# A graph-attention kernel on one core: scores in two groups of three units, and a new order of the work around them

## The chip, the core and the metric

One NeuronCore of a Trainium2 chip runs the whole kernel. The metric is the device time of one execution in microseconds (us). Five engines are spoken of: PE (TensorE, the matmuls; its weight loads are listed as PEld), DVE (VectorE), ACT (ScalarE), POOL (GpSimd), and SP (SyncE), which here only issues DMAs. Each engine runs its own list of instructions in order, and they meet through semaphores. Matmul results lie in eight PSUM banks of 128 partitions by 512 float32.

## What is computed

32 batches of 256 tokens with 384 features each; six heads of 64 features. The reference, cut to what matters:

```python
q = _heads(seq_inputs @ Wq + bq)
k = _heads(seq_inputs @ Wk + bk)
v = _heads(seq_inputs @ Wv + bv)
scores = jnp.einsum('bhqd,bhkd->bhqk', q, k) / np.sqrt(HEAD_SIZE)
bias = jnp.where(graph_mask, 0.0, NEG)[:, None]
probs = jax.nn.softmax(scores + bias, axis=-1)
ctx = jnp.einsum('bhqk,bhkd->bhqd', probs, v)
...
h = jnp.maximum(_layernorm(x, axis=-1), 0.0)
x = x + _L0_gnn_ref(h, L0_gnn_Wq, L0_gnn_bq, ..., adj)
```

## The kernel before

Every float32 matmul operand is split into an fp16 `hi` and an fp16 `lo` part, and a product is three fp16 matmuls (`three`: hi by hi, hi by lo, lo by hi). The work of a batch `b` is:

- `normalise` (POOL), `h_hi_rows` (ACT), `h_lo_rows` (DVE) and a DMA transpose `transpose_h` (SP) make the normalised input by columns, `h_cols`;
- `project_qk(b, j)`, 18 matmuls of 256 columns, makes q and k of head pair `j` (three pairs). `qk_full` (ACT) copies them out, `qk_hi_part` (DVE, a cast) and `split_lo` (POOL) split them into the tile `split`;
- `project_v(b, t)`, 9 matmuls of 384 columns, makes v of token half `t`; `v_hi_part` (ACT) and `v_lo_part` (DVE) split it;
- a **unit** `u` is one token half `t = u // 3` of one head pair `j = u % 3`, six in a batch. `scores` makes 12 matmuls for two units; each uses 64 of the 128 rows of the array, one for each head of the pair (`a` = 0, 1), and the two run side by side. `mask_and_max` (DVE, two instructions for a unit) masks them, `exps` and `probs_hi` (ACT) and `probs_lo` (POOL) make the probabilities, and `transpose_probs` (SP) turns them by DMA into `p_cols`;
- `apply_probs(b, u)`, 12 matmuls of 64 or 65 columns, sums the context of three units into the single bank `ctx`; `divide(b, t)` (DVE) takes it out, `transpose_context(b, t)` turns it on PE, `context_hi` (ACT) and `context_lo` (DVE) split it, `project_out(b, t)`, again 9 matmuls of 384 columns, multiplies by Wf, and `finish(b, t)` (DVE) adds the residual, which `add_bias` (POOL) has made. `store` (SP) writes it out.

The order on each engine is written out by hand. A start-up is followed by a function `cycle(b)` on each engine for b = 1 to 29, and by a hand-written end for the last two batches, `PREV` (30) and `LAST` (31). On PE a cycle scores batch b in three groups of two units (`scores(b, g)`), applies the last four units of b-1 and the first two of b, and projects b+1. All buffers are shared over batches with two, three or four copies. The score banks are two (`score_bank[a]`), so the next group may be written only when `mask_and_max` has read the one before (`logits_ready`). The first group of a cycle needs the splits of head pairs 0 and 1 (`qk_lo_ready`), the second that of pair 2 as well.

Two waits return below. `apply_probs(b, 0)` and `apply_probs(b, 3)` overwrite the one context bank and so wait for the `divide` before them. And DVE and POOL both read and write SBUF: `qk_hi_part` and `h_lo_rows` last longer beside POOL work.

## Time and profile before

| | us |
|---|---|
| median of 3 runs (589.86 to 590.72) | 590.62 |
| the profiled execution, its own time | 591.8 |
| its span, first to last instruction | 590.0 |
| start-up, until the scores of batch 2 start | 64.0 |
| 28 cycles, batches 2 to 29 | 485.3 |
| the end, from the scores of batch 30 on | 40.8 |
| PE busy share, mean granted clock | 97%, 0.996 |

How to read it: the trace gives each instruction's start and duration. Matmuls overlap, so what one costs is the distance from its start to the next one's start, not its duration. A busy share says little on DVE, ACT and POOL; what matters is whether their chain delivers before PE gets to the instruction that needs it. A cycle here means the time from the first scores matmul of one batch to that of the next.

### The profile page before, as it was taken

How to read it: one execution, taken by the hardware profiler on the slowest of the kernel's cores; microseconds unless marked ns; L12 is line 12 of the kernel's file. 1: busy time of each engine (PE TensorE's matmuls, PEld its weight loads, DVE VectorE, ACT ScalarE, POOL GpSimd, SP SyncE). 2: the span in 40 equal slices, each digit the busy share in tenths (PEclk: the TensorE clock that was granted, in tenths of full speed). 3: DMA queues.
4: the chain of work that ended last, by engine and by line, in shares of the span. 5: the costliest groups of instructions: out<-in, count | busy, mean ns of one | idle time of the engine just before them, and what ended most of it. 6: DMA issues, size and time to landing. Idle time of an engine off the chain costs nothing.

```text
span 590.0 us, 17760 instructions
## 1 busy us (share of the span) xinstructions
PE 573.5 (97%) x6640; PEld 428.9 (73%) x6640; DVE 473.8 (80%) x1484; ACT 516.1 (87%) x1161; POOL 491.3 (83%) x533
## 2 busy tenths in 40 slices
PE   7997999999999999999999999999999999999977
PEld 7676777777777777777777777777777777777755
DVE  4988788888888888878888887887877778787775
ACT  1788999899999999999999999999999999999882
POOL 2779998888998888899888889988888988888960
PEclk9999999999999999999999999999999999999999
DMA  8047889788888978899988877899988788987584
GB/s 273 10 77 140 133 169 184 158 169 167 156 156 165 176 162 168 174 129 174 179 167 170 162 169 150 158 183 156 183 162 159 151 159 181 160 157 143 72 162 117
DMA packets 275641, 92.01 MB, mean 156 GB/s; under 512 B 257634, under 2 KB 275555, under 8 KB 275555
## 3 DMA queue, kind: packets, MB, share of 16 engines
q1 hardware_dynamic: 274352, 90.87, 79.6%
q8 instruction: 53, 0.87, 0.6%
q14 instruction: 34, 0.27, 0.1%
q10 hardware_dynamic: 1202, 0.01, 0.1%
HBM read 17.05 MB, written 12.58 MB: 50 GB/s over the span
## 4 chain that ended last, share of the span: by engine, by line
PE 80%; DVE 6%; ACT 5%; DMA 5%; issue 2%; POOL 2%; ACTq 0%; SPq 0%; DVEq 0%; POOLq 0%
PE ring L1106 18%; PE ring L1108 18%; PE ring L1107 18%; PE scores L1169 11%; PE ctx L1195 5%; PE ring L1207 3%; PE ctx L1197 3%; PE ctx L1196 3%; DMA p_cols<-p_rows 3%; ACT probs L574 2%; DVE logits L796 1%; DVE h_rows L813 1%; DMA bf_row<-in_L_gnn_bf_dram 1%; ACT qk L602 1%; POOL p_rows L440 1%
## 5 line engine op out<-in xcount | busy, mean ns | idle before, releaser
L440 POOL TENSOR_TENSOR p_rows<-probs,p_rows 128x512 f16<-128x512 f32 x190 | 220.6, 1161 | 30.2 <-ACT p_rows L582 29.8
L796 DVE CUSTOM_DVE_ANT_0 logits<-scores,mask,logit_unscale 128x256 f32<-128x256 f32 x384 | 169.1, 478 | 57.5 <-PE scores L1169 57.3
L574 ACT ACTIVATE probs<-logits,raised 128x256 f32<-128x256 f32 x372 | 168.9, 501 | 6.1
L1106 PE MATMUL ring<-h_cols,w_hi 128*128 128x256 f16 x576 | 157.2, 273 | 0.0
L1108 PE MATMUL ring<-h_cols,w_lo 128*128 128x256 f16 x576 | 157.0, 273 | 0.0
L1107 PE MATMUL ring<-h_cols,w_hi 128*128 128x256 f16 x576 | 156.9, 272 | 0.0
L426 POOL TENSOR_TENSOR split<-qk,split 128x512 f16<-128x512 f32 x96 | 111.4, 1160 | 36.4 <-DVE split L820 36.4
L582 ACT ACTIVATE p_rows<-probs 128x512 f16<-128x512 f32 x190 | 119.6, 630 | 5.9
L602 ACT ACTIVATE qk<-ring,qk_bias_s,qkv_ratio 128x256 f32<-128x256 f32 x192 | 96.5, 552 | 3.9 <-PE ring L1108 3.8
L1195 PEld LDWEIGHTS ctx<-v_hi,p_cols 128*128 128x128 f16 x756 | 69.0, 97 | 33.9 <-issue 26.1
L1195 PE MATMUL ctx<-v_hi,p_cols 128*128 128x65 f16 x756 | 88.1, 195 | 5.5 <-DMA p_cols<-p_rows 4.1
L1196 PE MATMUL ctx<-v_lo,p_cols 128*128 128x64 f16 x756 | 87.6, 192 | 0.0
L1197 PE MATMUL ctx<-v_hi,p_cols 128*128 128x65 f16 x756 | 87.6, 193 | 0.0
L820 DVE CAST split<-qk 128x512 f16<-128x512 f32 x96 | 64.8, 675 | 27.4 <-ACT qk L602 27.1
L570 ACT ACTIVATE raised<-least,p_raise 128x2 f32<-128x2 f32 x186 | 54.3, 292 | 32.9 <-DVE least L796 31.8
L1169 PE MATMUL scores<-split 64*128 64x256 f16 x1152 | 79.5, 271 | 3.2 <-DVE least L796 2.5
L1169 PEld LDWEIGHTS scores<-split 64*128 64x128 f16 x1152 | 48.4, 94 | 31.7 <-issue 18.8
L1196 PEld LDWEIGHTS ctx<-v_lo,p_cols 128*128 128x128 f16 x756 | 69.6, 98 | 2.5
L1197 PEld LDWEIGHTS ctx<-v_hi,p_cols 128*128 128x128 f16 x756 | 69.7, 97 | 0.0
L435 POOL TENSOR_TENSOR residual<-x_in,bf_full 128x384 f32<-128x384 f32 x64 | 68.0, 1081 | 0.0
L1106 PE MATMUL ring<-w_hi,h_cols 128*128 128x384 f16 x192 | 62.6, 326 | 0.7 <-DVE w_lo L895 0.7
L1106 PE MATMUL ring<-w_hi,ct_hi 128*128 128x384 f16 x192 | 62.8, 327 | 0.0
(116 smaller groups left out, 1155.7 us busy)
## 6 DMA issues: line engine op xcount, KB each, us to landing
x_in<-in_x_dram SPq DMA_DIRECT2D x32, 384.0 KB, 3.8
out_dram<-result SPq DMA_DIRECT2D x62, 192.0 KB, 2.2
p_cols<-p_rows SPq DMA_TRANSPOSE x190, 3.2
adj_in<-in_adj_dram SPq DMA_DIRECT2D x32, 64.0 KB, 2.6
w_raw<-in_L_gnn_Wq_dram SPq DMA_DIRECT2D x1, 576.0 KB, 6.1
w_raw<-in_L_gnn_Wv_dram SPq DMA_DIRECT2D x1, 576.0 KB, 7.9
w_raw<-in_L_gnn_Wf_dram SPq DMA_DIRECT2D x1, 576.0 KB, 9.0
h_cols<-h_rows SPq DMA_TRANSPOSE x29, 4.8
```

The costliest lines, as they stand in the source:

```text
L426: pool.tensor_tensor(split[b.parity][j][:, 0:4:3, :], qk32[j][:], split[b.parity][j][:, 1:3, :], ALU.subtract).then_inc(qk_lo_ready, 1)
L440: pool.tensor_tensor(p_rows[u][:, 1], probs[u % 3][:], p_rows[u][:, 0], ALU.subtract).then_inc(p_lo_ready, 1)
L574: act.activation(probs[u % 3][:, a], logits[u % 3][:, a], ACT.Exp, bias=raised[u % 3][:, a:a + 1], scale=-1.0).then_inc(probs_ready, 1)
L582: act.activation(p_rows[u][:, 0], probs[u % 3][:], ACT.Copy).then_inc(p_hi_ready, 1)
L796: dve.tensor_tensor_reduce(out=logits[u % 3][:, a], in0=score_bank[a][:, u % 2 * S:(u % 2 + 1) * S], in1=mask[b.parity][:, t], scale=logit ...
L1106: pe.matmul(out_ap, a_hi, m_hi, start=first, stop=False)
L1107: pe.matmul(out_ap, a_hi, m_lo, start=False, stop=False)
L1108: return pe.matmul(out_ap, a_lo, m_hi, start=False, stop=last)
L1169: mm = pe.matmul(score_bank[a][:, u % 2 * S:(u % 2 + 1) * S], tile[own, q, t * P:(t + 1) * P], tile[own, k], start=(n == 0), stop=(n == 2))
L1195: pe.matmul(ctx_ps[:, h], hi, vh, start=(s == 0), stop=False)
L1196: pe.matmul(ctx_ps[:, h, 0:D], hi, vl, start=False, stop=False)
L1197: mm = pe.matmul(ctx_ps[:, h], lo, vh, start=False, stop=(s == QT - 1))
```

## The change

Scores come in two groups of three units. They use three banks, the third being the one that held the peaks of the weights at the start: heads 0 of units 1 and 2 share a bank, heads 1 of units 0 and 1 share another, and the third bank holds head 0 of unit 0 and head 1 of unit 2. These last two lie on different rows of the array, so the first matmul of unit 2's head 1 waits for unit 0's head 0 by a new semaphore, `shared_bank_done`, which PE sets for itself. All three splits of a batch are now needed at the start of its first group. The order in `cycle` is new on every engine: on SP the next input's load is the last of the cycle; on POOL `probs_lo` of unit 0 comes ahead of `root` and `normalise`, and that of unit 2 ahead of `split_lo(b + 1, 0)`, `split_lo(b + 1, 2)` goes ahead of `probs_lo(b, 4)` and `add_bias` last. Batch 1 has a PE order of its own, with a projection between the applied units. Batch 0 is scored in four groups (0 and 1; 2; 3; 4 and 5). The end is in another order too, with other banks for its context and output. In the diff the pieces behind the first `cycles` are, in this order, the cycles of SP, POOL, ACT and DVE, and then PE.

```diff
-    GROUPS = UNITS // 2
+    GROUPS = UNITS // C
...
-        score_bank = [bank("scores0"), bank("scores1")]
-        peak_bank = bank("peaks")
+        score_bank = [bank(f"scores{n}") for n in range(3)]
+        peak_bank = score_bank[2]
...
+        shared_bank_done = sem("shared_bank_done")
...
-        last_pt = {4: ring[2], 5: score_bank[0]}
+        last_pt = {4: ring[2], 5: score_bank[2]}
...
+        def score_of(u, a):
+            n, column = ((1, 0), (2, 0), (0, 0), (2, S), (0, S), (1, S))[u % C * 2 + a]
+            return score_bank[n][:, column:column + S]
...
-            return ring[3] if t == 1 and b.k >= B - 2 else ring[1]
+            return ring[2] if t == 1 and b.k == B - 1 else ring[1]
...
+        def ct_of(b, t):
+            return (score_bank[0] if b.k == B - 1 else ring[1]) if t == 0 else ring[0]
...
-            bank = peak_bank if b.k == B - 1 and t == 0 else ctx_bank
+            bank = ring[3] if b.k == B - 1 and t == 0 else ctx_bank
...
-        def cycles(cycle):
-            for k in range(1, B - 2):
+        def cycles(cycle, first=1):
+            for k in range(first, B - 2):
                 cycle(Batch(k))
...
@@ -325,37 +342,24 @@
...
+                transpose_probs(b + -1, 4)
+                transpose_probs(b + -1, 5)
                 if (b + -2).exists():
                     store(b + -2, 0)
-                if before:
-                    transpose_probs(b + -1, 5)
-                if here:
-                    transpose_probs(b, 0)
+                transpose_probs(b, 0)
                 if (b + -2).exists():
                     store(b + -2, 1)
-                if here and (b + 4).exists():
+                if (b + 3).exists():
+                    wait(sp, mask_ready, (b + 1).count(2, 2))
+                    load_adj(b + 3)
+                transpose_probs(b, 1)
+                transpose_probs(b, 2)
+                transpose_h(b + 2)
+                transpose_probs(b, 3)
+                if (b + 4).exists():
                     wait(sp, residual_ready, b.count(2, 2))
                     load_x(b + 4)
...
@@ -494,40 +498,22 @@
...
+                probs_lo(b, 0)
+                root(b + 2)
+                normalise(b + 2)
+                make_mask(b + 1)
+                probs_lo(b, 1)
+                probs_lo(b, 2)
+                split_lo(b + 1, 0)
+                split_lo(b + 1, 1)
+                probs_lo(b, 3)
+                split_lo(b + 1, 2)
+                probs_lo(b, 4)
+                add_bias(b + 1)
 
...
@@ -671,46 +657,27 @@
...
+                exps(b, 0)
+                probs_hi(b, 0)
+                v_hi_part(b, 1)
+                exps(b, 1)
+                probs_hi(b, 1)
+                qk_full(b + 1, 0)
+                context_hi(b + -1, 0)
+                exps(b, 2)
+                probs_hi(b, 2)
+                h_hi_rows(b + 2)
+                qk_full(b + 1, 1)
+                exps(b, 3)
+                probs_hi(b, 3)
+                qk_full(b + 1, 2)
+                exps(b, 4)
+                context_hi(b + -1, 1)
+                probs_hi(b, 4)
+                exps(b, 5)
+                v_hi_part(b + 1, 0)
+                probs_hi(b, 5)
...
@@ -970,54 +937,34 @@
...
+                context_lo(b + -1, 0)
+                mask_and_max(b, 3)
+                divide(b + -1, 1)
+                h_lo_rows(b + 2)
+                qk_hi_part(b + 1, 1)
                 if (b + 3).exists():
                     layer_stats(b + 3, (1,))
+                mask_and_max(b, 4)
+                if (b + 3).exists():
                     layer_moments(b + 3)
-                if here:
-                    mask_and_max(b, 5)
-                if before:
-                    finish(b + -1, 0)
-                    context_lo(b + -1, 1)
+                qk_hi_part(b + 1, 2)
+                mask_and_max(b, 5)
+                context_lo(b + -1, 1)
+                finish(b + -1, 0)
 
...
-            def scores(b, g):
-                for u in (2 * g, 2 * g + 1):
+            def scores(b, units):
+                for u in units:
                     if u < C:
                         wait(pe, qk_hi_ready, b.count(C, u + 1))
                         wait(pe, qk_lo_ready, b.count(C, u + 1))
-                wait(pe, logits_ready, b.count(2 * UNITS, 4 * g))
-                for u in (2 * g, 2 * g + 1):
+                wait(pe, logits_ready, b.count(2 * UNITS, 2 * units[0]))
+                for u in units:
                     t, tile = u // C, split[b.parity][u % C]
                     for n, (q, k) in enumerate(((1, 2), (1, 3), (0, 2))):
                         for a in range(2):
+                            if u % C == 2 and n == 0 and a == 1:
+                                wait(pe, shared_bank_done, b.count(GROUPS, u // C + 1))
                             own = slice(D * a, D * a + D)
-                            mm = pe.matmul(score_bank[a][:, u % 2 * S:(u % 2 + 1) * S],
-                                           tile[own, q, t * P:(t + 1) * P], tile[own, k],
+                            mm = pe.matmul(score_of(u, a), tile[own, q, t * P:(t + 1) * P], tile[own, k],
                                            start=(n == 0), stop=(n == 2))
+                            if u % C == 0 and n == 2 and a == 0:
+                                mm.then_inc(shared_bank_done, 1)
                 mm.then_inc(scores_ready, 1)
...
-                if t == 0 and (b + -1).exists():
-                    wait(pe, result_ready, (b + -1).count(2, 2 if b.k < B - 1 else 1))
+                if t == 0 and b.k == B - 1:
+                    pe.wait_ge(logits_ready, b.count(2 * UNITS, 2 * UNITS))
+                elif t == 0 and (b + -1).exists():
+                    wait(pe, result_ready, (b + -1).count(2, 2))
...
-            scores(Batch(0), 1)
+            scores(Batch(0), (2,))
             project_v(Batch(0), 1)
             bias_product(range(1, C))
             project_qk(Batch(1), 0)
             pe.wait_ge(peak_ready, 6)
             pe.wait_ge(peaks_joined, 2)
-            spread_peaks(peak_bank, slice(5, 6))
+            spread_peaks(ring[1], slice(5, 6))
+            scores(Batch(0), (3,))
             project_qk(Batch(1), 1)
-            scores(Batch(0), 2)
+            scores(Batch(0), (4, 5))
             project_qk(Batch(1), 2)
...
+            scores(Batch(1), (0, 1, 2))
+            apply_probs(Batch(0), 2)
+            project_qk(Batch(2), 0)
+            apply_probs(Batch(0), 3)
+            project_qk(Batch(2), 1)
+            apply_probs(Batch(0), 4)
+            transpose_context(Batch(0), 0)
+            scores(Batch(1), (3, 4, 5))
+            apply_probs(Batch(0), 5)
+            project_qk(Batch(2), 2)
+            apply_probs(Batch(1), 0)
+            pe.wait_ge(w_lo_ready, 8)
+            project_out(Batch(0), 0)
+            project_v(Batch(2), 0, (0,))
+            apply_probs(Batch(1), 1)
+            transpose_context(Batch(0), 1)
+            project_v(Batch(2), 0, (1, 2))
+            project_v(Batch(2), 1)
...
+                scores(b, (0, 1, 2))
+                apply_probs(b + -1, 2)
                 if (b + -2).exists():
                     project_out(b + -2, 1)
...
+                apply_probs(b + -1, 3)
+                project_qk(b + 1, 0)
+                apply_probs(b + -1, 4)
+                transpose_context(b + -1, 0)
+                project_qk(b + 1, 1)
+                scores(b, (3, 4, 5))
+                apply_probs(b + -1, 5)
+                project_qk(b + 1, 2)
+                apply_probs(b, 0)
+                project_out(b + -1, 0)
+                project_v(b + 1, 0, (0,))
+                apply_probs(b, 1)
+                transpose_context(b + -1, 1)
+                project_v(b + 1, 0, (1, 2))
+                project_v(b + 1, 1)
+            cycles(cycle, 2)
...
 
-            scores(PREV, 0)
+            scores(PREV, (0, 1, 2))
             apply_probs(PREV + -1, 2)
             project_qk(LAST, 0)
             project_out(PREV + -2, 1)
-            scores(PREV, 1)
+            scores(PREV, (3, 4, 5))
             apply_probs(PREV + -1, 3)
+            apply_probs(PREV + -1, 4)
             transpose_context(PREV + -1, 0)
-            apply_probs(PREV + -1, 4)
             project_qk(LAST, 1)
             apply_probs(PREV + -1, 5)
-            scores(PREV, 2)
             project_qk(LAST, 2)
             transpose_context(PREV + -1, 1)
+            project_v(LAST, 0, (0,))
             project_out(PREV + -1, 0)
-            project_v(LAST, 0, (0,))
+            project_v(LAST, 0, (1, 2))
+            scores(LAST, (0, 1, 2))
+            project_v(LAST, 1)
             apply_probs(PREV, 0)
-            scores(LAST, 0)
-            project_v(LAST, 0, (1, 2))
             apply_probs(PREV, 1)
-            project_v(LAST, 1)
             apply_probs(PREV, 2)
             project_out(PREV + -1, 1)
-            scores(LAST, 1)
+            scores(LAST, (3, 4, 5))
+            apply_probs(PREV, 3)
             transpose_context(PREV, 0)
-            scores(LAST, 2)
-            apply_probs(PREV, 3)
             apply_probs(PREV, 4)
+            project_out(PREV, 0)
             apply_probs(PREV, 5)
-            project_out(PREV, 0)
-            transpose_context(PREV, 1)
             apply_probs(LAST, 0)
             turn_probs(4)
+            transpose_context(PREV, 1)
+            apply_probs(LAST, 1)
             turn_probs(5)
-            apply_probs(LAST, 1)
             apply_probs(LAST, 2)
             project_out(PREV, 1)
```

Where the order moved, first **PE at the start of a cycle**: the end of `project_v`, the scores, and the first matmul of `apply_probs`. Before:

```order
L1108 MATMUL ring<-w_hi,h_cols 128x384
L1169 MATMUL scores<-split_0 128x256 [waits qk_lo_ready,qk_hi_ready,logits_ready]
L1169 MATMUL scores<-split_0 128x256 x5
L1169 MATMUL scores<-split_1 128x256 x6
L1195 MATMUL ctx<-v_hi,p_cols 128x65 [waits p_placed2]
```

And after:

```order
L1055 MATMUL ring<-w_hi,h_cols 128x384
L1120 MATMUL scores<-split_0 128x256 [waits qk_hi_ready,qk_lo_ready,logits_ready]
L1120 MATMUL scores<-split_0 128x256 x5
L1120 MATMUL scores<-split_1 128x256 x6
L1120 MATMUL scores<-split_2 128x256
L1120 MATMUL scores<-split_2 128x256 [waits shared_bank_done]
L1120 MATMUL scores<-split_2 128x256 x4
L1147 MATMUL ctx<-v_hi,p_cols 128x65 [waits p_placed2]
```

The third unit has joined the group, with a wait on PE's own semaphore between its first two matmuls.

Second, **DVE after the second group of the new cycle** (L763 is `mask_and_max`, L780 `h_lo_rows`, L787 `qk_hi_part`, L800 and L802 `divide`), from unit 3 to the cast of pair 2:

```order
L763 ISA logits0,least0<-scores1,mask1,logit_unscale 128x256
L763 ISA least0 128x1
L763 ISA logits0,least0<-scores2,mask1,logit_unscale 128x256
L763 ISA least0 128x1
L800 RECIPROCAL inv_sum1<-ctx 128x6
L802 TENSOR_TENSOR context1<-ctx,inv_sum1 128x384
L780 SCALAR_TENSOR_TENSOR h_rows<-normed,h_rows 128x3x128 x2
L787 CAST split0_1<-qk32_1 128x512
L826 BN_STATS stats<-x_in2 128x6
```

Before, the two `h_rows` instructions stood ahead of unit 3:

```order
L820 CAST split0_0<-qk32_0 128x512
L841 TENSOR_TENSOR ct_lo0<-ring1,ct_hi0 128x384
L813 SCALAR_TENSOR_TENSOR h_rows<-normed,h_rows 128x3x128 x2
L796 ISA logits0,least0<-scores0,mask1,logit_unscale 128x256
```

They now stand behind unit 3 and its `divide`, and ahead of the casts of pairs 1 and 2.

Third, **POOL in the second half of a cycle** (the lines with `p_rows` are `probs_lo`, those with `split1` are `split_lo`). Before:

```order
L440 TENSOR_TENSOR p_rows1<-probs1,p_rows1 128x512
L426 TENSOR_TENSOR split1_0<-qk32_0,split1_0 128x2x256
L440 TENSOR_TENSOR p_rows2<-probs2,p_rows2 128x512
L426 TENSOR_TENSOR split1_1<-qk32_1,split1_1 128x2x256
L440 TENSOR_TENSOR p_rows3<-probs0,p_rows3 128x512
L435 TENSOR_TENSOR residual3<-x_in3,bf_full 128x384 x2
L440 TENSOR_TENSOR p_rows4<-probs1,p_rows4 128x512
```

After:

```order
L444 TENSOR_TENSOR p_rows1<-probs1,p_rows1 128x512
L444 TENSOR_TENSOR p_rows2<-probs2,p_rows2 128x512
L430 TENSOR_TENSOR split1_0<-qk32_0,split1_0 128x2x256
L430 TENSOR_TENSOR split1_1<-qk32_1,split1_1 128x2x256
L444 TENSOR_TENSOR p_rows3<-probs0,p_rows3 128x512
L430 TENSOR_TENSOR split1_2<-qk32_2,split1_2 128x2x256
```

The split of pair 2 has moved up behind unit 3, and the residual has left the place between units 3 and 4 for the end of the cycle.

## Rows read from the trace of the kernel before

**Rows 1.** The page: busy us, share of the span and instructions of each engine

```profile
PE 573.5 (97%) x6640; PEld 428.9 (73%) x6640; DVE 473.8 (80%) x1484; ACT 516.1 (87%) x1161; POOL 491.3 (83%) x533
```

**Rows 2.** Windows: length; busy of PE, PEld, DVE, ACT, POOL; clock, DMA, GB/s

```profile
0.00:64.00 64.00, 55.17 (x505) 43.72 (x507) 50.58 (x145) 43.61 (x93) 44.39 (x60) 0.97 0.57 127
64.00:549.20 485.20, 484.22 (x5713) 360.38 (x5712) 396.12 (x1254) 445.55 (x1010) 425.38 (x449) 1.00 0.85 163
549.20:590.00 40.80, 34.06 (x426) 24.76 (x425) 27.09 (x85) 26.99 (x60) 21.53 (x26) 0.99 0.61 118
```

**Rows 3.** PE timeline (start, duration, what): first scores of batches 1, 2, 30

```profile
44.16 0.83 PE L1169 MATMUL scores<-split 64*128 64x256 f16 x12
...
63.96 0.83 PE L1169 MATMUL scores<-split 64*128 64x256 f16 x12
...
549.22 0.83 PE L1169 MATMUL scores<-split 64*128 64x256 f16 x12
```

**Rows 4.** PE timeline around the second scores group of batch 15

```profile
294.33 0.27 PE L1107 MATMUL ring<-h_cols,w_hi 128*128 128x256 f16 x1
294.44 0.27 PE L1108 MATMUL ring<-h_cols,w_lo 128*128 128x256 f16 x1
294.65 0.83 PE L1169 MATMUL scores<-split 64*128 64x256 f16 x12
295.41 0.20 PE L1195 MATMUL ctx<-v_hi,p_cols 128*128 128x65 f16 x1
```

**Rows 5.** DVE timeline in batch 15's cycle, in brackets the idle time before

```profile
295.52 0.48 DVE L796 CUSTOM_DVE_ANT_0 logits<-scores,mask,logit_unscale 128x256 f32<-128x256 f32 x1 [1.02 <-PE scores L1169]
...
298.25 1.43 DVE L813 SCALAR_TENSOR_TENSOR h_rows<-normed,h_rows 128x384 f16<-128x384 f32 x2
299.60 0.47 DVE L796 CUSTOM_DVE_ANT_0 logits<-scores,mask,logit_unscale 128x256 f32<-128x256 f32 x1
...
300.41 0.18 DVE L833 RECIPROCAL inv_sum<-ctx 128x6 f32<-128x6 f32 x1
...
301.10 0.42 DVE L820 CAST split<-qk 128x512 f16<-128x512 f32 x1
...
303.42 0.73 DVE L820 CAST split<-qk 128x512 f16<-128x512 f32 x1 [0.64 <-ACT qk L602]
304.07 0.55 DVE L859 BATCH_NORM_STATS2 stats<-x_in 128x6 f32<-128x384 f32 x1
304.54 0.29 DVE L865 BATCH_NORM_AGGREGATE mean_var<-stats 128x2 f32<-128x6 f32 x2
...
305.02 0.48 DVE L796 CUSTOM_DVE_ANT_0 logits<-scores,mask,logit_unscale 128x256 f32<-128x256 f32 x1
```

**Rows 6.** Operations of one tile: least, median and greatest duration in ns

```profile
L813 DVE SCALAR_TENSOR_TENSOR h_rows<-normed,h_rows x58: 543/580/1555, 53.8 to 541.3; 128x384 f16<-128x384 f32 x58
...
L820 DVE CAST split<-qk x96: 416/729/1311, 20.2 to 567.0; 128x512 f16<-128x512 f32 x96
L426 POOL TENSOR_TENSOR split<-qk,split x96: 1142/1158/1472, 20.7 to 567.9; 128x512 f16<-128x512 f32 x96
```

**Rows 7.** Landing time of `p_cols` over the run; PE timeline in batch 1's cycle

```profile
DMA to landing us min/median/max: 3.0/3.2/5.7
...
51.82 0.20 PE L1195 MATMUL ctx<-v_hi,p_cols 128*128 128x65 f16 x1 [1.79 <-DMA p_cols<-p_rows]
```

**Rows 8.** SP timeline at 46 us: the load of batch 4, then two transposes

```profile
45.71 0.37 SPq L283 DMA_DIRECT2D x_in<-in_x_dram  x1
46.13 2.90 SPq L297 DMA_TRANSPOSE p_cols<-p_rows  x2
```

**Rows 9.** Chain that ended last, from 549 us: the transpose of batch 30's unit 5

```profile
570.86 4.75 DMA p_cols<-p_rows
```

**Rows 10.** ACT and PE timelines: last exponentials; `apply_probs` of batch 31's unit 3

```profile
575.16 1.71 ACT L722 ACTIVATE probs<-logits,raised 128x256 f32<-128x256 f32 x4
...
581.28 0.19 PE L1195 MATMUL ctx<-v_hi,p_cols 128*128 128x65 f16 x1
```

249 lines of the change are left out of this document (63 added, 186 removed).

## The prediction, made before the changed kernel was run

> **What bounds the kernel now.** First the shares of busy time: PE 97%, ACT 87%, POOL 83%, DVE 80% [rows 1]. Such a share says little alone, so the windows by stage come next [rows 2]: over the 28 cycles of batches 2 to 29, PE is busy 484.2 of 485.2 us, at full clock. In the start-up it is busy 55.2 of 64.0, in the end 34.1 of 40.8. So 28 cycles are bound by what PE has to stream, and start-up and end hold some 16 us in which PE waits. Third, the starts of the first scores group of a batch [rows 3]: 63.96 for batch 2, 549.22 for batch 30, which is 485.26 / 28 = 17.33 us a cycle; batch 1 starts at 44.16, so its cycle takes 19.80. Last, PE's timeline around a scores group [rows 4]. The projection's matmuls start 0.11 us apart, but the scores start 0.21 after the last of them: 0.10 is lost on the way in. The group runs from 294.65 to the next start at 295.41, 0.76 us, while its six pairs at 0.11 are 0.66: 0.10 is lost on the way out. A group costs 0.20 us beside its work, and nothing hides that on the engine that bounds.
>
> **The cycle: one group fewer.** The same 36 score matmuls come in two groups. That takes away 0.20 us in each of 28 cycles, 5.6 us. The new cycle is 17.13 by the mean (17.33 less 0.20), if everything PE needs is in time. PE's order with starts from the first scores, made of the spacings (scores of three units 1.08, a head pair's projection 1.97, a value or output projection 1.47, `apply_probs` 0.36): `apply_probs(b-1, 2)` at 1.1, `project_out(b-2, 1)` 1.4, `apply_probs(b-1, 3)` 2.9, `project_qk(b+1, 0)` 3.3, `apply_probs(b-1, 4)` 5.2, `project_qk(b+1, 1)` 6.0, the second scores 8.05, `apply_probs(b-1, 5)` 9.1, `project_qk(b+1, 2)` 9.5, `apply_probs(b, 0)` 11.5, `project_out(b-1, 0)` 11.8, `apply_probs(b, 1)` 13.8, and the next batch's scores at 17.1.
>
> **The wait that moves up.** The first group now needs the split of head pair 2, which before was wanted only 5 us later. It hangs on DVE's new order behind the second scores. DVE sees a two-unit group 0.87 after its start (294.65 to 295.52 [rows 4, 5]), so a three-unit one after 0.87 + 3 x 0.11 = 1.20: 8.05 + 1.20 = 9.25. Then by starts [rows 5]: unit 3 0.81 (299.60 to 300.41), `divide` 0.69 (300.41 to 301.10), `h_lo_rows` 1.35 (298.25 to 299.60), cast of pair 1 0.34 (0.42 less the 0.08 by which neighbours overlap), one batch norm 0.47, unit 4 0.81, moments 0.48, together 4.95: 14.20. The cast of pair 2 takes 0.73 beside POOL, and 0.07 to POOL's start: 15.00. The split takes 1.16 [rows 6], 0.06 to PE: 16.2. PE wants it at 17.1: 0.9 us to spare. On the same engine unit 5, which frees the banks, is read by 14.20 + 0.65 + 0.81 + 0.15 = 15.8: 1.3 to spare. ACT is busy 445.55 / 28 = 15.9 of the 17.1 [rows 2] and stays below; POOL 425.38 / 28 = 15.2. `v_lo_part(b, 0)`, which frees the bank of `project_qk(b+1, 1)`, now stands behind unit 2: 1.20 + 3 x 0.81 + `divide` 0.69 + `finish` about 0.53 + its own 0.61 = 5.5 against 6.0. Nothing in the cycle is late by this, and what is queued behind the new wait on PE (all of the cycle) loses nothing.
>
> **The wait inside a group.** PE now waits for its own matmul: unit 0's last product for head 0 is the third pair, at 0.22, and its end is seen some 0.31 after its start (0.87 less the 0.55 at which the last pair of a two-unit group starts): 0.53. The waiting matmul is the seventh pair, at 0.66, and its weights load 0.11 ahead, at 0.55. No row shows such a wait, so bounds: 0 if the 0.02 holds; 0.10 if the array has to run empty once more, the price of leaving a group. The least is 0, since no work goes. I take 0, as the sum of the rows comes out just in time; 0.10 would be 2 x 28 x 0.10 = 5.6 us. The added increment costs no more: the last projection of a head pair carries one too, and its successor is not held. The Trainium skill (TensorE: Matmul & The Clock Gate, The cost: per-tile semaphore tail) says that increments of tiles serialise, about 26 ns each; by that, an estimate, 56 more of them would cost 1.5 us and the sum end at 582.5.
>
> **The SP queue.** The load of x moves from ahead of `transpose_probs(b, 1)` to behind `transpose_probs(b, 3)`, and so ahead of `transpose_probs(b, 4)`. That one is issued about 0.7 into the next cycle and wanted at 5.2, 4.5 later. Transposes land after 3.0 to 5.7, median 3.2 [rows 7]; the 5.7 is just of this kind, issued 0.42 behind a load of x [rows 8] and landing as 51.82 shows [rows 7]. Now the load is 1.3 ahead of it, so I take 4.0 and a late one here and there, 0.2 us in all; the ends are 0 and, if every one took 5.7, 1.2 x 28 = 34 us.
>
> **Start-up.** In batch 1's cycle PE now has two projections between units 2 and 4 of batch 0, where it stood for `divide` and for the late transpose of unit 4. The work of that cycle is 17.1 less the missing `project_out` of 1.5, 15.6. What stays: the transpose of unit 4, whose place on SP does not change, lands at 51.8, 7.7 after the cycle's start, while PE would be there at 5.7 without waits; of these 2.0 us, 1.2 go to `v_lo_part(1, 0)`, now behind unit 2, ahead of it. 15.6 + 2.0 = 17.6, and 0.2 for batch 0's extra group: 17.8 against 19.80, **2.0 us less**. It could be 1.0 (if the slowest `h_rows`, 1.555 us each [rows 6], comes again) or 3.5 (if the transpose landed in 3.2).
>
> **The end.** Before, the chain stands on the transpose of batch 30's unit 5, issued at 570.86 and landing 4.75 later [rows 9]. It is 21.6 us after batch 30's first scores. Now `probs_hi(PREV, 5)` comes ahead of the exponentials of batch 31, and the chain runs through ACT: from 2.2 us (1.20 for the scores, 1.0 for the first unit) six units of exponentials (1.27) with `probs_hi` (0.54), three `qk_full` (0.90), five copies (0.41), six exponentials of batch 31 (0.93; the last two in 1.71 [rows 10]) and four `probs_hi`, about 10.9 + 2.7 + 2.0 + 5.4 + 2.2 = 23.2: done at 25.4 if ACT never waits, against 575.16 + 1.71 - 549.22 = 27.65 now. Behind it stand PE's transpose, two applied units and a `project_out`, as now, until unit 3 of batch 31 at 581.28 - 549.22 = 32.1; what follows that is unchanged. So at most 2.3 us from this chain, and as the row of `p_cols` shows that landings go over 4, I take **2.0 us**; ends 0 and 4.
>
> **Sum.** 5.6 + 2.0 + 2.0 - 0.2 = 9.4 us. The profiled execution took 591.8 (span 590.0), so 582.4 for such a one; it lies 1.2 above the median of 590.62. Against the median: 581.2.
>
> **Rivals.** (A) *POOL beside DVE makes the split late.* `h_rows` takes 0.58 in the median and 1.555 at most, the cast 0.42 to 1.31 [rows 6]. In the rows of DVE the first of two `h_rows` took 0.97 (1.43 and the overlap of 0.08, less the free 0.54). If the second does too, +0.43, and the casts take 1.00 each (between the median of 0.73 and the most), +0.58 and +0.27, the split is there at 17.5, 0.4 late: 28 x 0.4 = 11.2 us, 592.4 and slower. It decides from 0.3 of lateness in each cycle, which eats the whole gain; against it speaks the 0.9 to spare, and that POOL itself waits for the cast of pair 1 and so leaves it alone. 8%. (A2) *Each cast is held for a whole POOL operation*: 1.16 ahead of the free 0.42 for both, 1.16 + 0.85 more than in the walk, 18.2, 1.1 late, 28 x 1.1 = 31 us and 612. Against it: the median of the casts is 0.73, so most are held for 0.3. 2%. The Trainium skill (SBUF — State Buffer, SBUF: two separate sides) gives the rule for this: the port that DVE shares with POOL is locked for a whole instruction and the other engine blocks. (B) *Transposes behind the load of x are late*, by 0.3 a cycle: 8.4 more, 589.6. For it the 5.7 [rows 7]; against it the wider distance. 8%. (C) *The wait inside a group costs* 0.1 each: 5.6 more, 586.8. 10%. (D) *Only the cycle gains*: in start-up and end other waits take the place of those removed, 4.0 more, 585.2. 12%. That the change doesn't do what it says is excluded by PE's order, which shows the groups.
>
> **How the numbers follow.** The forecast has 60%, with 577.0 to 585.0 for its own ends (2 us either way in start-up and end each never fall together, plus the odd landing). 577 to 588 holds nearly all of it with (C) and (D), 8 in 10. A measurement of this kernel can tell about 0.2%, 1.2 us, from no change. Faster by that, under 589.4: the forecast, (C), (D) and half of (B), 86%; within it, the other half of (B) and a little of (A), 5%; slower, the rest of (A) and (A2), 9%.
>
> **What would show it.** A cycle of 17.1 us between first scores, two groups with 0.1 lost on each side, PE's waits for `split` absent. Wrong if PE's list of waits names `split`, `least` or `p_cols` in the middle window for more than 3 us; if pairs six and seven of a group stand over 0.12 apart; if batch 1's cycle is over 18.5, or the end over 39.5.

## The result, and the profile of the changed kernel

The changed kernel takes 592.40 us (median of 6 runs, 592.12 to 593.62), the kernel before, run beside it, 590.65. The ratio is 1.0031, with a 95% interval of 1.0017 to 1.0046. So it is slower by 0.3%, where 581.2 was forecast, and outside the range of 577 to 588. The profiled execution has a span of 590.5 us against 590.0 before.

First the page's shares, to be held against [rows 1]:

```profile
PE 569.0 (96%) x6640; PEld 434.4 (74%) x6640; DVE 479.8 (81%) x1484; ACT 509.8 (86%) x1161; POOL 491.1 (83%) x533
```

TensorE is busy 4.5 us less (573.5 before), as part of the time lost around a group counts as busy and there are fewer groups, but the span has not shrunk with it. Where it went is in the windows by stage (length; then busy time of PE, PEld, DVE, ACT, POOL; clock, DMA share, GB/s), to be held against [rows 2]:

```profile
0.00:62.73 62.73, 54.97 (x503) 43.28 (x503) 49.78 (x145) 43.57 (x93) 43.18 (x59) 0.97 0.53 123
62.73:550.79 488.06, 480.13 (x5713) 366.27 (x5713) 402.79 (x1254) 439.14 (x1009) 424.92 (x449) 1.00 0.88 162
550.79:590.50 39.71, 33.87 (x426) 24.89 (x425) 27.23 (x85) 27.14 (x61) 23.05 (x27) 1.00 0.72 127
```

In the middle window PE is busy 480.13 of 488.06 us, so it now stands still for 7.9 us, against 1.0 before. The stage's borders are the first scores of batches 1, 2 and 30 on PE's timeline, as in [rows 3] (the last projection ahead of batch 2's is shown too):

```profile
43.80 0.39 PE L1120 MATMUL scores<-split 64*128 64x256 f16 x4
...
62.48 0.33 PE L1055 MATMUL ring<-w_hi,h_cols 128*128 128x384 f16 x1
62.73 0.39 PE L1120 MATMUL scores<-split 64*128 64x256 f16 x4
...
550.79 0.39 PE L1120 MATMUL scores<-split 64*128 64x256 f16 x4
```

| stretch | before | forecast | after |
|---|---|---|---|
| to batch 1's first scores | 44.16 | 44.16 | 43.80 |
| batch 1's cycle | 19.80 | 17.8 | 18.94 |
| cycles 2 to 29, mean | 17.33 | 17.13 | 17.43 |
| from batch 30's first scores to the end | 40.8 | 38.8 | 39.7 |

(The 17.8 holds 0.2 for batch 0's extra group.) The span that was forecast is 590.0 less 9.4, and the measured one, 590.5, is 9.9 us longer. Of these, 28 x 0.30 = 8.4, less the 0.2 that the forecast gave to the SP queue, lie in the cycles: 8.2. PE's list of waits in that window (who waited for whom: us in total, times, longest) names two causes:

```profile
PE scores L1120 <- POOL split L430: 5.0, 20, 0.3
PE ctx L1147 <- DMA p_cols<-p_rows: 2.9, 6, 0.6
```

Twenty of 28 times a batch's first scores wait for POOL's low part of the split, and six times the value products wait for a transpose. The prediction named both kinds of wait as its refutation ("for more than 3 us"); the first is over that alone. Two more of its signs came as well: batch 1's cycle is over 18.5 and the end over 39.5. PE's timeline at the second scores of batch 14 and at the first ones of batch 15:

```profile
279.91 1.16 PE L1120 MATMUL scores<-split 64*128 64x256 f16 x18
281.00 0.20 PE L1147 MATMUL ctx<-v_hi,p_cols 128*128 128x65 f16 x1
...
288.65 0.33 PE L1055 MATMUL ring<-w_hi,h_cols 128*128 128x384 f16 x1
289.23 0.39 PE L1120 MATMUL scores<-split 64*128 64x256 f16 x4 [0.26 <-POOL split L430]
```

The three-unit group runs from 279.91 to 281.00, 1.09 us: nine pairs at 0.11 are 0.99, and 0.10 is lost on the way out. That is what the forecast had (1.08). The wait inside the group stands ahead of the seventh pair, and in all 56 groups of the 28 cycles the trace has that pair 0.109 to 0.110 us behind the sixth, no farther than the other pairs are apart: it costs nothing. But the first scores of batch 15 start 0.58 us after the last projection, where those of batch 2 start 0.25 after it (62.48 to 62.73). Batch 14's first scores were at 289.23 - 17.37 = 271.86. Twenty of the 28 cycles take 17.36 or 17.37; one in which nothing is late takes 17.05. So the scores are 0.32 us late.

DVE's and POOL's timelines between the two groups tell why (rows of DVE, then of POOL; the rows x2 are two instructions in one):

```profile
281.11 0.48 DVE L763 CUSTOM_DVE_ANT_0 logits<-scores,mask,logit_unscale 128x256 f32<-128x256 f32 x1 [0.54 <-PE scores L1120]
...
282.63 2.00 DVE L780 SCALAR_TENSOR_TENSOR h_rows<-normed,h_rows 128x384 f16<-128x384 f32 x2
284.55 0.42 DVE L787 CAST split<-qk 128x512 f16<-128x512 f32 x1
284.88 0.55 DVE L826 BATCH_NORM_STATS2 stats<-x_in 128x6 f32<-128x384 f32 x1
285.35 0.47 DVE L763 CUSTOM_DVE_ANT_0 logits<-scores,mask,logit_unscale 128x256 f32<-128x256 f32 x1
...
286.15 0.24 DVE L832 BATCH_NORM_AGGREGATE mean_var<-stats 128x2 f32<-128x6 f32 x2
286.43 0.92 DVE L835 TENSOR_SCALAR var_s<-mean_var 128x2 f32<-128x2 f32 x1
287.26 0.15 DVE L837 TENSOR_SCALAR neg_mean<-mean_var 128x2 f32<-128x2 f32 x1
287.33 0.41 DVE L787 CAST split<-qk 128x512 f16<-128x512 f32 x1
```

```profile
282.59 1.15 POOL L430 TENSOR_TENSOR split<-qk,split 128x512 f16<-128x512 f32 x1
285.04 1.16 POOL L430 TENSOR_TENSOR split<-qk,split 128x512 f16<-128x512 f32 x1 [1.30 <-DVE split L787]
286.16 1.16 POOL L444 TENSOR_TENSOR p_rows<-probs,p_rows 128x512 f16<-128x512 f32 x1
287.82 1.16 POOL L430 TENSOR_TENSOR split<-qk,split 128x512 f16<-128x512 f32 x1 [0.50 <-DVE split L787]
```

POOL's split of pair 0 starts 0.04 us ahead of DVE's first `h_rows`, and the two `h_rows` take 1.92 us to the next start instead of about 1.0. It is the first one alone that is held: over the cycles the first takes 1.53 us in the median and the second 0.55. POOL's `p_rows` of unit 3 starts at 286.16, and `var_s`, a `tensor_scalar` of two numbers in each partition, starts at 286.43 and ends at 287.35, with POOL's operation (287.32). The batch norm beside POOL's split (284.88) and the unit's logits, which read PSUM, take no longer than elsewhere. Both delays lie ahead of the cast of pair 2, and POOL's split of pair 2 waits for that cast: POOL stands idle 0.50 us just ahead of it, so POOL's own work is not what makes it late. This is not an accident of one cycle, as the operations' durations over the middle of the run show (least/median/greatest in ns; the kernel before first, then the changed one):

```profile
L868 DVE TENSOR_SCALAR var_s<-mean_var x27: 168/170/903, 79.2 to 529.8; 128x2 f32<-128x2 f32 x27
```

```profile
L780 DVE SCALAR_TENSOR_TENSOR h_rows<-normed,h_rows x55: 544/707/1536, 73.5 to 544.5; 128x384 f16<-128x384 f32 x55
L835 DVE TENSOR_SCALAR var_s<-mean_var x27: 912/919/925, 77.3 to 530.7; 128x2 f32<-128x2 f32 x27
L787 DVE CAST split<-qk x82: 411/415/429, 70.0 to 541.0; 128x512 f16<-128x512 f32 x82
```

`var_s` went from 170 ns to 919, in every batch. The casts, for which the prediction feared POOL, went the other way, from 729 [rows 6] to 415. The Trainium skill (SBUF — State Buffer, Who interferes with whom) says which DVE operations want the ports that POOL uses: those with two inputs in SBUF against a POOL operation that reads it, and copies, casts and `tensor_scalar` where they enter a two-port mode; whoever starts first has them for the whole instruction. The rows agree: `h_rows` and `var_s` are held until POOL's operation ends, the logits and the statistics are not. `var_s` is over 0.03 us behind that end; `h_rows`, which takes 0.55 by itself, 0.4 us behind it.

### The profile page after: what moved, and what is told of

It reads as the page before. It is cut to its first block, busy times and chain, and to the rows that moved or that the text cites. A ratio compares the mean times of both kernels' runs of the same rounds, so it can differ in the third digit from the quotient of the medians.

```text
span 590.5 us, 17761 instructions
## 1 busy us (share of the span) xinstructions
PE 569.0 (96%) x6640; PEld 434.4 (74%) x6640; DVE 479.8 (81%) x1484; ACT 509.8 (86%) x1161; POOL 491.1 (83%) x533
## 3 DMA queue, kind: packets, MB, share of 16 engines
HBM read 17.05 MB, written 12.58 MB: 50 GB/s over the span
## 4 chain that ended last, share of the span: by engine, by line
PE 50%; DVE 17%; POOL 14%; issue 9%; DMA 7%; ACT 1%; ACTq 0%; POOLq 0%; DVEq 0%
PE ring L1053 10%; PE ring L1055 10%; PE ring L1054 10%; PE scores L1120 9%; DMA p_cols<-p_rows 6%; DVE logits L763 5%; POOL p_rows L444 5%; POOL split L430 4%; DVE h_rows L780 3%; PE ctx L1147 3%; DVE split L787 2%; POOL residual L439 2%; PE ring L1161 2%; DVE context L802 2%; PE ctx L1149 2%
## 5 line engine op out<-in xcount | busy, mean ns | idle before, releaser
L763 DVE CUSTOM_DVE_ANT_0 logits<-scores,mask,logit_unscale 128x256 f32<-128x256 f32 x384 | 168.6, 477 | 48.7 <-PE scores L1120 48.6
L1120 PE MATMUL scores<-split 64*128 64x256 f16 x1152 | 74.4, 270 | 5.8 <-POOL split L430 5.6
L787 DVE CAST split<-qk 128x512 f16<-128x512 f32 x96 | 41.9, 436 | 41.5 <-ACT qk L588 41.4
L1120 PEld LDWEIGHTS scores<-split 64*128 64x128 f16 x1152 | 53.3, 94 | 27.5 <-issue 24.2
L439 POOL TENSOR_TENSOR residual<-x_in,bf_full 128x384 f32<-128x384 f32 x64 | 62.8, 1003 | 0.0
```

Source lines behind the costliest of these rows:

```text
L763: dve.tensor_tensor_reduce(out=logits[u % 3][:, a], in0=score_of(u, a), in1=mask[b.parity][:, t], scale=logit_unscale[:, 0:1], scalar=FAR, ...
L1120: mm = pe.matmul(score_of(u, a), tile[own, q, t * P:(t + 1) * P], tile[own, k], start=(n == 0), stop=(n == 2))
```

## Experiments

The theory (T): POOL's operations hold `h_lo_rows` and `var_s`, so that the split of pair 2 comes 0.32 us after TensorE wants it. Rivals: (R1) the wait inside a three-unit group, or the group itself, eats the gain; (R2) late transposes on the reordered SP queue. Each edit is against the changed kernel, if nothing else is said. Ratios are to the kernel before, run on the same chip beside them (its medians there were 590.65 beside after, 591.15 beside e1 to e4, 592.57 beside e5, e6, f1 and f2, 591.52 beside the others), with the 95% interval; compare rows by their ratios. The usual cycle is the commonest distance between the first scores of two batches in the profiled execution.

| kernel | median us | ratio | usual cycle | waits for the split of pair 2 |
|---|---|---|---|---|
| after | 592.40 | 1.0031 [1.0017, 1.0046] | 17.36 | 20 |
| e1, wait for pair 2 two units later | 588.31 | 0.9949 [0.9930, 0.9969] | 17.05 | none |
| e2, moments behind unit 5 | 589.17 | 0.9971 [0.9953, 0.9988] | 17.09 | none listed |
| e3, SP's order as before | 593.78 | 1.0042 [1.0028, 1.0055] | 17.36 | 19 |
| e4, POOL's split of pair 0 short | 585.99 | 0.9905 [0.9878, 0.9931] | 17.05 | none |
| e5, only `var_s`, `neg_mean` later | 591.74 | 0.9991 [0.9972, 1.0010] | 17.23 | 0.19 each |
| e7, POOL's `p_rows` of unit 3 short | 585.32 | 0.9891 [0.9859, 0.9923] | 17.05 | none |
| e6, e1 and unit 1's transpose first | 583.69 | 0.9853 [0.9824, 0.9883] | 17.05 | none |
| e8, e6 with one more group | 595.99 | 1.0071 [1.0047, 1.0094] | 17.62 | none |
| f1, e6 with DVE and ACT reordered | 601.95 | 1.0156 [1.0132, 1.0181] | 17.83 | none |
| f2, f1 with the load of x later | 601.93 | 1.0156 [1.0131, 1.0180] | 17.83 | none |
| g1, e6 with the load of x later | 580.45 | 0.9814 [0.9789, 0.9840] | 17.05 | none |
| g2, g1 with start-up and end changed | 581.62 | 0.9827 [0.9802, 0.9852] | 17.05 | none |

**e1: the wait for pair 2 stands before unit 2.**

```diff
-                for u in units:
-                    if u < C:
-                        wait(pe, qk_hi_ready, b.count(C, u + 1))
-                        wait(pe, qk_lo_ready, b.count(C, u + 1))
                 wait(pe, logits_ready, b.count(2 * UNITS, 2 * units[0]))
                 for u in units:
+                    if u < C:
+                        wait(pe, qk_hi_ready, b.count(C, u + 1))
+                        wait(pe, qk_lo_ready, b.count(C, u + 1))
```

> The changed kernel, with TensorE's waits for the split of head pair j moved from the head of the scores group to just before unit j's own matmuls, so the wait for pair 2 stands two units, 2 x 0.33 = 0.66 us, later. Theory T (the split of pair 2 is 0.32 us late, since DVE's chain behind the second scores is held by POOL): the stall at the start of a batch's first scores is covered, so the usual cycle falls from 17.36 to 17.04 us, and 28 cycles with the odd late transpose take 21 to 28 times 0.32 = 7 to 9 us less: 583.5 to 586 us. Rival R1 (the wait of a matmul inside the group for its own group's matmul is what costs, or the three-unit group itself): nothing changes, 592. Rival R2 (late transposes): the usual cycle stays 17.36, 592.

Measured: 588.31 us, and the usual cycle is 17.05. PE's list of waits in the 28 cycles has one line left:

```profile
PE ctx L1146 <- DMA p_cols<-p_rows: 5.1, 9, 0.8
```

The stall at the scores is gone, by 0.32 a cycle as expected, so R1 falls: the same groups with the same own-semaphore wait run in 17.05. The total gained 4.1 us by the medians (4.8 by the ratios) and not 7 to 9, as the late transposes went from 2.9 us in six waits to 5.1 in nine. From start to start, the value products of unit 1 lose 3.1 us, about as in the changed kernel (3.3), and those of unit 4 lose 3.8, where they lost 0.9. Unit 4's products stand behind the scores that were late, so that lateness had given its transpose 0.32 us more.

**e2: the moments leave the chain.**

```diff
                 mask_and_max(b, 4)
-                if (b + 3).exists():
-                    layer_moments(b + 3)
                 qk_hi_part(b + 1, 2)
                 mask_and_max(b, 5)
+                if (b + 3).exists():
+                    layer_moments(b + 3)
```

> The changed kernel, with layer_moments(b+3) moved on DVE from behind unit 4's mask_and_max to behind unit 5's, so that the two aggregations and the two tensor_scalars, one of which lasts 0.92 us beside a POOL operation, no longer stand ahead of the cast of pair 2. Theory T: the cast then starts when ACT's qk of pair 2 is there, up to 1.2 us earlier, so the first scores are in time: cycle 17.05, 583.5 to 586 us; unit 5 comes no later. Within T, if the held h_lo_rows alone is the cause and ACT's qk is the later one, it gains nothing. Rivals R1 and R2: no change, 592.

Measured: 589.17 us, usual cycle 17.09; the mean cycle is 17.34, with nine odd ones up to 18.46 from transposes (5.9 us). That is the theory's cycle within 0.04; the total again falls short of it by the transposes. The place shows the contention from its other side, on POOL's and then DVE's timeline:

```profile
303.25 1.43 POOL L444 TENSOR_TENSOR p_rows<-probs,p_rows 128x512 f16<-128x512 f32 x1
304.64 1.15 POOL L430 TENSOR_TENSOR split<-qk,split 128x512 f16<-128x512 f32 x1
```

```profile
303.25 0.41 DVE L787 CAST split<-qk 128x512 f16<-128x512 f32 x1
304.39 0.23 DVE L832 BATCH_NORM_AGGREGATE mean_var<-stats 128x2 f32<-128x6 f32 x2
304.66 1.16 DVE L835 TENSOR_SCALAR var_s<-mean_var 128x2 f32<-128x2 f32 x1
```

Here the cast and POOL's `p_rows` start together, and it is POOL that takes 0.27 us more while the cast has its free 0.41. `var_s` then starts just behind POOL's split and lasts 1.16, the whole of it.

**e3: SP's cycle in the order of before.**

```diff
+                if (b + 4).exists():
+                    wait(sp, residual_ready, b.count(2, 2))
+                    load_x(b + 4)
+                transpose_probs(b, 1)
+                transpose_probs(b, 2)
+                transpose_h(b + 2)
                 if (b + 3).exists():
                     wait(sp, mask_ready, (b + 1).count(2, 2))
                     load_adj(b + 3)
-                transpose_probs(b, 1)
-                transpose_probs(b, 2)
-                transpose_h(b + 2)
                 transpose_probs(b, 3)
-                if (b + 4).exists():
-                    wait(sp, residual_ready, b.count(2, 2))
-                    load_x(b + 4)
```

> The changed kernel, with the order of the SP queue's cycle as in the kernel before: the load of x ahead of the transpose of unit 1, the load of adj ahead of that of unit 3. Theory T: the usual cycle stays at 17.36; of the 0.07 us a cycle that lies above it (the odd wait for p_cols, 2 us in all) some may go or come; 590 to 594 us. Rival R2 (what the reordered queue costs is what eats the gain): the cycle falls to 17.1, 585 us.

Measured: 593.78 us, usual cycle 17.36, 19 waits for the split and 5.1 us of waits for transposes. The old order of the queue is no faster here, so R2 falls as the main cause. The trace also has each transpose's time from issue to landing. With the load of x back ahead of unit 1's transpose, that one takes 3.7 us in the median (3.3 in the changed kernel), and unit 4's, which the load has left, 3.05 (3.8 in the changed kernel).

**e4: POOL's split of pair 0 made short** (most of the low parts of pair 0 are left out).

```diff
+                n = 32 if j == 0 and 1 < b.k < B - 2 else S
-                pool.tensor_tensor(split[b.parity][j][:, 0:4:3, :], qk32[j][:], split[b.parity][j][:, 1:3, :],
-                                   ALU.subtract).then_inc(qk_lo_ready, 1)
+                pool.tensor_tensor(split[b.parity][j][:, 0:4:3, 0:n], qk32[j][:, :, 0:n],
+                                   split[b.parity][j][:, 1:3, 0:n], ALU.subtract).then_inc(qk_lo_ready, 1)
```

> The changed kernel, with POOL's low part of the split of pair 0 cut in the cycles from 256 to 32 columns of each half, so that the low parts of most keys and queries of pair 0 are left out: POOL's operation falls from 1.16 to about 0.2 us. Theory T: the first h_lo_rows, which starts beside it, falls from 1.5 to about 0.6 us, the split of pair 2 comes up to 0.9 us earlier, and the first scores are in time: cycle 17.05 us, 583.5 to 586 us; if the 0.92 of the tensor_scalar stays and takes the saving, the cycle stays at 17.36. Rivals R1 and R2: no change, 592.

**e7: POOL's `p_rows` of unit 3 made short** (most of its low parts are left out), the same for the other collision.

```diff
+                n = 32 if u == 3 and 1 < b.k < B - 2 else S
-                pool.tensor_tensor(p_rows[u][:, 1], probs[u % 3][:], p_rows[u][:, 0],
-                                   ALU.subtract).then_inc(p_lo_ready, 1)
+                pool.tensor_tensor(p_rows[u][:, 1, :, 0:n], probs[u % 3][:, :, 0:n], p_rows[u][:, 0, :, 0:n],
+                                   ALU.subtract).then_inc(p_lo_ready, 1)
```

> The changed kernel (without the late wait), with POOL's low part of unit 3's probabilities cut in the cycles from 256 to 32 columns of each half, so that most of those low parts are left out: the POOL operation beside which DVE's var_s lasts 0.92 us falls from 1.16 to about 0.3. Theory T (whatever DVE issues while that POOL operation runs is held to its end): var_s takes 0.2 to 0.4, the cast behind it stays at 0.42, the split of pair 2 comes 0.5 to 0.7 earlier and the cycle of 17.36 becomes 17.05: 586 to 588 us with the odd late transposes. Rival (the two small operations are slow by themselves in this place, for instance as they wait for the aggregation's result): var_s stays at 0.92 and the cycle at 17.36, 592 us.

Measured: 585.99 and 585.32 us, both with a usual cycle of 17.05 and no wait for the split. In e4 the first `h_rows` of a cycle falls from 1.53 to 0.68 us, while `var_s` stays at 0.92; in e7 it is `h_rows` that stays, at 1.53. The row of `h_rows` in e4 (both of a cycle together), and that of `var_s` in e7:

```profile
L781 DVE SCALAR_TENSOR_TENSOR h_rows<-normed,h_rows x56: 543/549/1524, 73.4 to 540.5; 128x384 f16<-128x384 f32 x56
```

```profile
L836 DVE TENSOR_SCALAR var_s<-mean_var x27: 168/170/171, 77.2 to 523.6; 128x2 f32<-128x2 f32 x27
```

DVE's own instructions, their order and their shapes are those of the changed kernel; only a POOL operation got shorter, and `var_s` is back at 170 ns (below the 0.2 to 0.4 expected). So it is not slow by its place or its inputs. Each collision costs more than the 0.32 us by which the split is late, so it takes both to make it late, and taking either away suffices. As part of POOL's work is left out, the totals are no version to use.

**e5: only the two small operations move behind the cast.**

```diff
-                dve.wait_ge(moments, b.count(4, 4))
-                wait(dve, norm_ready, b.count(2, 0))
+                if b.k < 4:
+                    layer_scalars(b)
+
+            def layer_scalars(b):
+
+                dve.wait_ge(moments, b.count(4, 4))
+                wait(dve, norm_ready, b.count(2, 0))
...
                 qk_hi_part(b + 1, 2)
+                if (b + 3).exists():
+                    layer_scalars(b + 3)
                 mask_and_max(b, 5)
```

> The changed kernel, with only the two small tensor_scalars of layer_moments(b+3) (var_s and neg_mean; one lasts 0.92 us where 0.17 is its free time) moved behind the cast of pair 2 on DVE; the aggregations stay, and so does the h_rows of 1.5 us beside POOL's split of pair 0. Theory T: the chain gets 0.9 to 1.0 us shorter, so the split of pair 2 is in time in every cycle: the cycle of 17.36 becomes 17.05, and with the odd late transposes as in the two kernels before the total is 586 to 589 us. Rival: the small operation takes the delay only in place of the cast behind it (POOL's p_rows operation has to end anyway before DVE goes on), so the cast of pair 2 lasts 0.75 longer instead: the cycle stays at 17.36 and the total at 592.

Measured: 591.74 us, usual cycle 17.23. The rival had the mechanism and came within 0.3 us of the total; the 586 to 589 of the theory was wrong. DVE's timeline in one cycle:

```profile
304.64 0.24 DVE L832 BATCH_NORM_AGGREGATE mean_var<-stats 128x2 f32<-128x6 f32 x2
304.80 1.29 DVE L787 CAST split<-qk 128x512 f16<-128x512 f32 x1
```

The cast takes 1.29 us instead of 0.41: it has stepped into the place of `var_s` beside POOL's `p_rows`, which runs from 304.66 to 305.82, and is done 0.27 us behind its end. Only `var_s`'s and `neg_mean`'s own time, some 0.13 of the cycle, is saved, and the waits for transposes ate it (5.0 us in nine, against 2.9 in six). So the delay belongs to the moment, not to the instruction; `var_s` was merely the first that wanted the ports. What helped was a cast that starts no later than POOL's operation (e2), or a shorter POOL operation (e4, e7).

**e6: e1, with unit 1's probabilities and their transpose first.**

```diff
-                make_mask(b + 1)
                 probs_lo(b, 1)
+                make_mask(b + 1)
...
+                transpose_probs(b, 1)
                 if (b + 3).exists():
                     wait(sp, mask_ready, (b + 1).count(2, 2))
                     load_adj(b + 3)
-                transpose_probs(b, 1)
```

> The late wait of e1, and on POOL the low part of unit 1's probabilities ahead of the mask, on SP its transpose ahead of the load of adj, so that this transpose is issued some 1.1 us earlier in each cycle. Theory U (the late wait gave back less than 9 us because transposes that land after 4.4 to 5 instead of 3.2 us are late for the value products of unit 1 by 0.65 to 0.96, five times, and for unit 4 by 0.3 to 0.9, six times): the five of unit 1 go, 4 us, and the 1.36 us for which TensorE waits for the same unit in batch 1's cycle: 588.3 - 5 = 583 us. Rival: the slow landings follow what else the queues carry and fall on the next transpose instead (units 2, 4): 586 to 588 us.

Measured: 583.69 us. The waits for transposes in the 28 cycles are 2.5 us in four, three of them for unit 4, one for unit 2 and none for unit 1, and the cycle of batch 1 takes 18.02 instead of 19.14 in e1. The rival, that a slow landing would fall on the next transpose instead, holds for one of 0.6 us.

**g1: e6, with the load of x behind unit 4's transpose**, and the statistics that need it later on DVE.

```diff
                 transpose_probs(b + -1, 4)
+                if (b + 3).exists() and b.k > 1:
+                    load_x(b + 3)
                 transpose_probs(b + -1, 5)
...
                 transpose_probs(b, 3)
                 if (b + 4).exists():
                     wait(sp, residual_ready, b.count(2, 2))
-                    load_x(b + 4)
...
-                if (b + 3).exists():
-                    layer_stats(b + 3, (0,))
                 qk_hi_part(b + 1, 0)
                 v_lo_part(b, 1)
                 if b.k == 1:
                     weights_lo(3, 8)
                 context_lo(b + -1, 0)
+                if (b + 3).exists():
+                    layer_stats(b + 3, (0,))
```

> The kernel with the late wait and unit 1 first (583.7 us), with the load of x issued behind unit 4's transpose instead of ahead of it, and the statistics that need it behind context_lo(b-1, 0) on DVE. Theory U (unit 4's transpose is slow since it runs beside the 384 KB of x): its landing falls from 3.7 to 3.1-3.3 us, the waits for it (0.94, 0.42 and 1.10 and some small ones in the cycles) go, and the total is 580.5 to 581.5 us. Rival: they are slow by what else the queues carry, and the waits stay or move to units 0 and 5: 583.5 us.

Measured: 580.45 us, 0.9814 of the kernel before and just where it was expected. Its middle window, and all that PE waited for in it:

```profile
62.89:540.90 478.01, 477.65 (x5714) 364.67 (x5714) 405.89 (x1256) 439.91 (x1011) 426.06 (x450) 1.00 0.92 166
```

```profile
PE ctx L1147 <- DMA p_cols<-p_rows: 0.2, 1, 0.2
```

PE is busy 477.65 of 478.01 us, and 478.01 / 28 = 17.07 is the cycle: the one fewer group is now worth its full 28 x 0.20 and somewhat more (17.33 - 17.07 = 0.26, since the odd late cycles of before went too). This is the fastest version of all that were run.

It also shows one cause of slow transposes. In e6 unit 4's takes 3.7 us in the median from issue to landing and 5.1 at most; here, with the load of x behind it, 3.06 and 3.6. Units 5 and 0, which now come next behind the load, go from 3.05 and 3.1 to 3.95 and 4.1, and PE hardly waits for them. Before the change it was unit 1's, just behind the load, that took 4.2.

**g2: g1, with two more edits.**

```diff
                 divide(b + -1, 0)
+                if b.k == 1:
+                    v_lo_part(b, 0)
                 mask_and_max(b, 1)
...
                 mask_and_max(b, 2)
-                v_lo_part(b, 0)
+                if b.k > 1:
+                    v_lo_part(b, 0)
...
+            apply_probs(PREV, 5)
             project_out(PREV, 0)
-            apply_probs(PREV, 5)
```

> g1 with two more edits: in batch 1's cycle v_lo_part(1, 0) ahead of unit 1 on DVE, so that TensorE's wait of 1.21 us for it at 47.5 goes; at the end apply_probs(30, 5) ahead of project_out(30, 0), where TensorE waited 0.97 us. Expected: the first gives 0.5 to 1.2 us unless the late unit 4 of batch 0 takes it back (TensorE waits for its transpose right behind, 1.0 us; then 0); the second 0 to 0.8: together 0.5 to 1.5 us below g1, 580 us. Rival: both waits only move behind, no gain over g1.

Measured: 581.62 us, an interval that overlaps that of g1, and the cycle of batch 1 takes 18.26 against 18.25. The rival holds: PE no longer waits for `v_lo_part(1, 0)`, and waits that much more for the transposes of batch 0. The end takes 39.35 against 39.25: the wait ahead of `project_out(30, 0)` shrinks by 0.6 us, and the next one for a transpose grows by 0.5.

**e8: one more group per cycle**, on e6.

```diff
-                wait(pe, logits_ready, b.count(2 * UNITS, 2 * units[0]))
+                wait(pe, logits_ready, b.count(2 * UNITS, 2 * (units[0] if b.k < 2 else units[0] // C * C)))
...
-                mm.then_inc(scores_ready, 1)
+                if b.k < 2 or units[-1] % C == C - 1:
+                    mm.then_inc(scores_ready, 1)
...
-                scores(b, (0, 1, 2))
+                scores(b, (0, 1))
                 apply_probs(b + -1, 2)
+                scores(b, (2,))
```

> The kernel with the late wait and unit 1 first (583.7 us), with its first scores group cut in two by apply_probs(b-1, 2) between units 1 and 2, both parts released together at the end, so that only one more change between scores and other matmuls is made per cycle. Theory (a group costs 0.20 us beside its work): the cycle goes from 17.05 to 17.25, 28 x 0.20 = 5.6 us more, 589.3 us. Rival (part of what a group costs is taken by its releases and not by the change of shape): less than 0.10 a cycle, 583.7 to 586.5 us. DVE sees the group 0.56 later, which may add late cycles: above 591 would show that.

Measured: 595.99 us, cycle 17.62, 0.57 more than e6. The late cycles that the expectation allowed for came in every one. PE's waits in the 28 cycles:

```profile
PE ctx L1147 <- DVE context L802: 6.1, 28, 0.2
```

DVE sees the group 0.56 us later and its `divide` is late for `apply_probs(b-1, 3)`. From start to start PE loses 0.38 there in each cycle (the list counts 0.22 of it as idle, since the last matmul's tail counts as busy). 0.57 - 0.38 = 0.19 is left for the group itself: the 0.20 of the forecast, shown now by adding one.

**f1 and f2: DVE's cycle reordered**, on e6; f2 has g1's edit besides.

```diff
-                h_lo_rows(b + 2)
                 qk_hi_part(b + 1, 1)
-                if (b + 3).exists():
-                    layer_stats(b + 3, (1,))
+                h_lo_rows(b + 2)
                 mask_and_max(b, 4)
-                if (b + 3).exists():
-                    layer_moments(b + 3)
                 qk_hi_part(b + 1, 2)
                 mask_and_max(b, 5)
+                if (b + 3).exists():
+                    layer_stats(b + 3, (1,))
+                    layer_moments(b + 3)
                 context_lo(b + -1, 1)
...
                 exps(b, 4)
-                context_hi(b + -1, 1)
                 probs_hi(b, 4)
+                context_hi(b + -1, 1)
```

> e6 with DVE's and ACT's order changed as well: the cast of pair 1 ahead of h_lo_rows (it then stands at 12 us of the cycle, beside no POOL operation of its own making), statistics and moments behind unit 5, ACT's context_hi(b-1, 1) behind unit 4's probs_hi. Theory T and U: no chain behind the second scores is late any more, and unit 4's transpose is issued 0.4 to 0.5 us earlier, which takes most of its six late ones (3.5 us) away: 580 to 583 us. Rival: h_rows, later by 0.4, make the transpose of h late, or the moments behind unit 5 push context_lo(b-1, 1) past TensorE's project_out(b-1, 1) at 1.4 of the next cycle: 585 to 590 us.

> f1 with the load of x issued behind unit 4's transpose instead of ahead of it, and the first statistics of x, which need it, behind context_lo(b-1, 0). Theory U: unit 4's transpose, which lands after 3.7 us with the load ahead of it, lands after 3.1 to 3.3, so that its late ones go wholly: 580 to 581 us; unit 5's, behind the load now, has 5 us to spare. Rival: the load then slows unit 0's and unit 5's transposes, with no gain over f1, or statistics wait for x: 583 us.

Measured: 601.95 and 601.93 us. PE's waits in f1 name the reason:

```profile
PE ring L1052 <- DVE result L817: 15.8, 26, 1.1
PE ctx L1145 <- DMA p_cols<-p_rows: 0.6, 1, 0.6
```

`project_out(b-1, 1)`, 1.4 us into the next cycle, waits for `finish(b-1, 0)`, the last in DVE's cycle, which the statistics and moments now push back. I had named the neighbour, `context_lo`, as the rival's cause, and taken 585 to 590 for its price; it was 18 us. The totals tell nothing of f2's load, as both hang on this one wait. The landings do, and as in g1: unit 4's transpose takes 4.0 us in the median in f1 and 3.07 in f2, unit 5's 3.1 and 3.8.

## Why the prediction was wrong, point by point

**One group fewer, 5.6 us: right.** The three-unit group takes 1.09 us, and a cycle in which nothing is late takes 17.05 against 17.26 to 17.30 in most cycles of before. e8 prices a group at 0.19 by adding one.

**The wait inside a group, 0: right.** e1 keeps it and loses nothing. The 17.05 is 17.26 less 0.21. The prediction counted 56 increments more; each cycle has two of `shared_bank_done` more but one of `scores_ready` less, so 28 more. By the Trainium skill (TensorE: Matmul & The Clock Gate, The cost: per-tile semaphore tail), at about 26 ns each, 56 would have cost an estimated 1.5 us (and the sum would have been 582.7, not 582.5), and 28 an estimated 0.7. No run here shows such a cost, and 0.03 us a cycle is too little for these rows to exclude it.

**The split of pair 2 at 16.2 of 17.1: this step failed.** It came at 17.37, and PE wanted it at 17.05. The walk had the right order and the right start: second scores at 8.05 (279.91 - 271.86), DVE's start at 9.25 (281.11). By its terms, read from the timelines above:

| term | forecast | measured |
|---|---|---|
| `h_lo_rows`, two | 1.35 | 1.92 (282.63 to 284.55) |
| moments | 0.48 | 1.18 (286.15 to 287.33) |
| cast of pair 2, to POOL's start | 0.80 | 0.49 (287.33 to 287.82) |
| POOL's split, to PE's start | 1.22 | 1.41 (287.82 to 289.23) |

+0.57, +0.70, -0.31 and +0.19 are +1.15, and with rounding that is 17.37. The two large ones are POOL's work beside DVE; e4 takes away the first of them and e7 the second, and either alone brings back the cycle of 17.05. The mistake was to read a duration off an operation in the old order and to carry it into the new one. `var_s` was taken at its usual 0.17, without asking what POOL does at that time in the new order, and `h_rows` and the casts at what POOL had made of them before. The rival (A) had the mechanism, the place and by luck the very total, 592.4, with 8%. Its sum put the delay on the casts, which came out free, and on the second `h_rows`, where the first alone is held, longer. Against itself it said that POOL leaves the chain alone as it waits for pair 1's cast; POOL does wait for it, and then runs two operations in a row, the second beside `var_s`. The 0.06 us from POOL's end to PE's start had no row behind it and is 0.25. 20 x 0.32 = 6.4 us is the price, more than the 5.6 us that one group fewer gives.

**The SP queue, 0.2: this step failed too.** The sum of cycles 2 to 29 holds 488.06 - 28 x 17.05 = 10.7 us above the undisturbed ones, of which 6.4 are the split and 4.3 odd late transposes, where before had 485.26 - 28 x 17.26 = 2.0 us above its undisturbed cycles. 3.3 of the 4.3 are unit 1's transpose, whose neighbour on SP is now the load of adj. That transpose was not costed: issued 9.67 into the cycle it lands in the usual 3.3 at 13.0, and PE wants it at 13.8, so one that takes 4.7 is late; the longest took 4.8. The other 0.9 are unit 4's, behind the load of x, for which the 0.2 stood. The landing that the prediction took, 4.0, was near (3.8 in the median, 5.1 at most). But in e1, with no stall at the scores, it is issued 1.2 into the next cycle and not 0.7, so it has 4.05 us and not 4.5; there unit 4 costs 3.8 us and unit 1 3.1. So the late split hid part of this error: with the split in time and nothing else changed, e1 takes 588.31, which is also outside the range. Rival (B), transposes behind the load of x, was right in kind and at 0.9 us here and 3.8 in e1 too dear at 8.4. e6 issues unit 1's earlier, g1 besides takes the load from ahead of unit 4's, and the listed waits come to 0.2 us.

**Start-up, -2.0: got -0.9 in batch 1's cycle.** Another 0.4 lies ahead of it (44.16 to 43.80), but kernels with the same start-up code have 43.5 to 44.2 there, so that is not shown to be a gain. The list of PE's idle times in batch 1's cycle, on its timeline:

```profile
48.80 0.28 PE L1053 MATMUL ring<-h_cols,w_hi 128*128 128x256 f16 x1 [1.05 <-DVE v_lo L791]
...
55.80 0.19 PE L1147 MATMUL ctx<-v_hi,p_cols 128*128 128x65 f16 x1 [0.61 <-DVE context L802]
...
59.47 0.20 PE L1147 MATMUL ctx<-v_hi,p_cols 128*128 128x65 f16 x1 [1.20 <-DMA p_cols<-p_rows]
```

From start to start PE loses 1.2 us for `v_lo_part(1, 0)`, as forecast. The wait for unit 4's transpose, 0.8 in the forecast, did not come: its products start at 50.77, 0.11 behind the projection ahead of them. Overlooked were 0.8 us for `divide` and 1.4 for the transpose of unit 1 of batch 1. The work of 15.6 and these 3.4 are 19.0 against 18.94. The 0.2 of batch 0's extra group does not belong here, since all of batch 0's groups stand ahead of batch 1's first scores; 17.8 was put together from terms that partly made up for each other. In e6, where unit 1's transpose goes first, the cycle takes 18.02.

**The end, -2.0: here -1.1.** 38.8 was forecast and 39.7 measured. The profiled executions of twelve kernels that end alike have 38.7 to 39.7 there, ten of them within 0.5 of the forecast. In this one batch 31's first transpose was issued at 572.20 and its products started at 577.20, after 1.03 us idle.

**Together**: 8.2 in the cycles, 1.1 in batch 1's, 0.9 in the end, less 0.4 ahead of batch 1: 9.8 of the 9.9 us. The time that the split left to spare was given as 0.9 us of a walk of 8 us in which two instructions were known to swing by 1 us; the 60% for "nothing is late" did not follow from such a margin.

What stays open is a part of the slow transposes. A load of x just ahead is one cause (e3, f2, g1). Others, of units 1 and 2, take 4.4 to 5.5 us with no load of x ahead of them, several at the same batches in several kernels, and no run shows why. e6 both took the load of adj from ahead of unit 1's and issued it 0.9 us earlier, so it does not tell whether the load of adj slowed it. Nor do the two costs simply add up: of the eight cycles that do not end in the full stall, six hold a late transpose of unit 1 and one a late one of unit 4, so PE was behind already.

## What to carry to other kernels

The duration of a DVE operation that shares ports with POOL belongs to the moment and not to the operation: when an order changes, write DVE's and POOL's rows of the new order beside each other, and price each DVE operation in a chain by what POOL runs at that time, small ones too. Here a margin of 0.9 us was less than one POOL operation, 1.16 us, and two of them fell into the chain. Check the DMA queue in the same way, for every transfer whose neighbour or place changes: from the changed kernel to e1 unit 4's transpose had 0.32 us less room, and its late landings cost 3.8 us instead of 0.9. And a wait that stands at the head of a group of matmuls can move to the first matmul that needs it: here two units later, and 0.32 us a cycle came back.

## What the runs showed of the hardware

- A `tensor_scalar` of 128x2 numbers takes 0.17 us by itself, 0.92 beside POOL's 1.16 us operation that started 0.27 earlier (after), and 1.16 where it starts just behind POOL (e2); it is back at 0.17 when POOL's operation is made short (e7). The delay did not shrink with the size of the DVE operation: 0.75 us here, 0.88 for a cast of 128x512 at the same place (e5).
- Moving the held operation away hands its delay to the next one that wants the ports: the cast went from 0.41 to 1.29 us (e5). Statistics and the logits' reads of PSUM were not held.
- Where the two start at the same time on the trace, POOL pays: 1.43 instead of 1.16 us beside a cast that takes its free 0.41 (e2).
- TensorE's wait for its own matmul, four pairs before the waiting one, costs nothing (0.109 us between pairs there as elsewhere), and changing between scores and other matmuls costs 0.19 to 0.21 us per group (e8; 17.26 less 17.05).
- A DMA transpose that lands after 3.05 to 3.3 us in the median takes 3.7 to 4.2 when 384 KB of x are issued just ahead of it (before, after, e3, e6, f1, f2, g1).
